# Cross-attention scores of a decoder layer: three float32r products of high and low parts, or one float32 product

## The chip, the cores and the metric

The kernel runs on one core of one Trainium2 chip. The metric is device time in microseconds (us) of that core, the median of several runs. The profile is of one further execution.

## The reference

One decoder layer over 8 requests of 128 tokens with 128 features: causal self-attention with 16 heads of 64, cross-attention with 16 heads of 8 on a context of 128 tokens, and a feed-forward of 8 experts with 256 hidden values of which two are chosen per token. After each of the three comes a residual and a layer norm. What the change touches is the cross-attention:

```python
qh = _split_heads(q @ Wq.T + bq, B, S)      # B=8, S=128, 16 heads of 8
kh = _split_heads(k @ Wk.T + bk, B, S)
vh = _split_heads(v @ Wv.T + bv, B, S)
scores = jnp.einsum('bhqd,bhkd->bhqk', qh, kh) / np.sqrt(DK)
scores = jnp.where(mask[:, None, :, :] == 0, NEG, scores)
attn = jax.nn.softmax(scores, axis=-1)
out = jnp.einsum('bhqk,bhkd->bhqd', attn, vh)
```

## The kernel before

Every engine has its own instruction stream, with the order of all calls written out by hand (there is no planner); semaphores tie the streams together. The attention of the 8 requests runs as a software pipeline: self-attention of request n, cross-attention of request n-1 or n-2 and the products of coming requests are interleaved call by call on each engine. After it the experts run in four chunks of 256 tokens. All eight PSUM banks (X0, X1, Y0, Y1, T0, T1, OS, OC) are handed from call to call by name; a call may write a bank once its last reader is done.

Many of the products are made from split operands: a value is held as a high part in float32r and a low part in float32r (value minus high part), and the product is the sum of three float32r products, high by high, high by low and low by high (`split_product`, lines 1441 to 1445; the projections at 1461 to 1465 and 1482 to 1484). Others, such as the transposes (L1545), the self-attention scores (L1527), the sums over keys (L1554 and L1563), the output projection (L1595) and the down products (L2043, L2053), are plain float32. In the trace each float32 product has two matmul records and two weight loads.

The cross scores, by which the change is told:

- `project_kc` (L1486, two calls) makes the keys of four requests at a time. `evac_kc` on ACT (L554) copies them to the high part `k_all[:, 0]` with their bias, and `lower_kc` on DVE (L823) writes the low part `k_all[:, 1]`. `k_all` lies in the memory of `down_sb`, the 1 MB of down weights, so that SP loads these weights only when the last of the 8 requests has used its keys (`sp.wait_ge(k_own_done, B)`, L272; the load is L273).
- `own_k` on POOL (L320) spreads the keys of one request, high and low part in one instruction each, over four column blocks and keeps in each block one head of each strip: `k_own`.
- `project_qc` (L1606) makes the queries of one request; `evac_qc` on DVE (L940) writes the high part `qc[:, 0]`, `lower_qc` on DVE (L828) the low part `qc[:, 1]`, out of the same bank.
- `score_c` on PE (L1538), 8 calls, one for each request: for each of four strips of 32 rows (8 features of 4 heads) three float32r products of 128 queries by 512 columns (4 heads by 128 keys) into the strip's own bank. That is 12 matmuls a call. It waits for `cq_evac`, `k_own_done` and `cq_lower`.
- `group_max` on DVE (L839) adds the mask to each strip's scores and takes the maxima; `exp` on ACT (L528) follows.

PE waits for `kc_lower` twice and for `cq_lower` once more ahead of calls that reuse a bank which `lower_kc` or `lower_qc` reads. DVE makes the mask (`spread_mask`, L818) once, from data that ACT's queue loads (L605); `x_tok`, which the residuals read, comes on the same queue (L609). SP's queue loads the weights: `gateT` and `upT` (L270, L271) are its last loads before `down`.

Of the kernel before, what the change touches and what calls it, by code (L numbers as in the profile page):

```python
# [5 lines left out]
F32 = mybir.dt.float32  # L6
F32R = mybir.dt.float32r
# [6 lines left out]
P = 128  # L14
# [24 lines left out]
def build_decoder(nc, x, xT, ctxT, mask, wqT, wkT, wvT, woT, cwqT, cwkT, cwvT, cwoT, cbq, cbk, cbv, cbo,  # L39
# [34 lines left out]
    with ExitStack() as ctx:  # L74
# [36 lines left out]

        k_all = down_sb[:].rearrange("p k d -> p (k d)").bitcast(F32R).rearrange("p (a t) -> p a t", a=2)

        ident = sb("ident", [P, P])
# [23 lines left out]
        ctx_lo = sb("ctx_lo", [P, B * S], F32R)  # L138
        k_own = sb("k_own", [P, 2, 2, 4, S], F32R)
        qc = sb("qc", [P, 2, S], F32R)  # L140
        cv_all = sb("cv_all", [P, B, D])
# [68 lines left out]
        def hid_of(b):  # L210
# [6 lines left out]
                             "bias_step bias_then_mean").split()]  # L217
        qk_first, qk_first_a, qk_first_v, kc_proj, kc_evac, kc_lower, cv_proj, cv_evac, k_own_done, cvp_done = [
            sem(n) for n in "qk_first qk_first_a qk_first_v kc_proj kc_evac kc_lower cv_proj cv_evac k_own_done cvp_done".split()]
        qk_proj, qk_evac = [[sem(f"{n}{i}") for i in range(4)] for n in ("qk_proj", "qk_evac")]  # L220
# [8 lines left out]
        (wo_s, res1_done, stat1_done, aggr1_done, var1_done, pow1_done, x1_ready, x1bo_done,  # L229
         x1T_ps, x1T_evac, cq_proj, cq_evac, cq_lower) = [sem(n) for n in (  # L230
             "wo_s res1_done stat1_done aggr1_done var1_done pow1_done x1_ready x1bo_done "
             "x1T_ps x1T_evac cq_proj cq_evac cq_lower").split()]
        (oc_evac, oct_ps, rec_c, ccat_done, ccatT_ps, ccatT_evac, wo_c, res2_done, stat2_done, aggr2_done, var2_done, pow2_done,
# [14 lines left out]
        @block.sync  # L248
        def _(sp):
            sp.dma_start(xT_all[:, 0:2 * S], xT[:, 0:2 * S]).then_inc(ld_xT, 16)  # L250
            sp.dma_start(w_raw[:, 1, W_COLS[0]], wkT[:, W_COLS[0]]).then_inc(ld_wqk[1], 16)
            for k in range(1, len(W_COLS)):
                sp.dma_start(w_raw[:, 0, W_COLS[k]], wqT[:, W_COLS[k]]).then_inc(ld_wqk[2 * k], 16)
            sp.dma_start(w_raw[:, 2, :], wvT).then_inc(ld_wv, 16)
            sp.dma_start(xT_all[:, 2 * S:B * S], xT[:, 2 * S:B * S]).then_inc(ld_xT_rest, 16)
            sp.dma_start(ctxT_all[:], ctxT).then_inc(ld_ctx, 16)
            sp.dma_start(cwqk_raw[:, 1], cwkT).then_inc(ld_cwk, 16)
            sp.dma_start(cwv_sb[:], cwvT).then_inc(ld_cw, 16)
            sp.dma_start(cwo_sb[:], cwoT).then_inc(ld_cw, 16)
            sp.dma_start(cb[:, 0], cbq).then_inc(ld_cw, 16)  # L260
            sp.dma_start(cb[:, 1], cbk).then_inc(ld_cw, 16)
            sp.dma_start(part[:], parts).then_inc(ld_cw, 16)
            sp.dma_start(cbrow[:, 0, :], cbv.rearrange("(a d) -> a d", a=1).broadcast_to([P, D])).then_inc(ld_cw, 16)
            sp.dma_start(cbrow[:, 1, :], cbo.rearrange("(a d) -> a d", a=1).broadcast_to([P, D])).then_inc(ld_cw, 16)
            sp.dma_start(router_sb[:], routerT).then_inc(ld_cw, 16)
            sp.dma_start(cwqk_raw[:, 0], cwqT).then_inc(ld_cwq, 16)
            sp.dma_start(wo_sb[:], woT).then_inc(ld_wo, 16)

            sp.wait_ge(w_lo_done, NWP)
            sp.dma_start(gu_raw[:, 0, :], gateT).then_inc(ld_gu, 16)  # L270
            sp.dma_start(gu_raw[:, 1, :], upT).then_inc(ld_gu, 16)  # L271
            sp.wait_ge(k_own_done, B)  # L272
            sp.dma_start(down_sb[:], down).then_inc(ld_down, 16)  # L273

            for c in range(NCH):
                for tb in range(TB):
                    b = c * TB + tb
                    sp.wait_ge(y_ready, b + 1)
                    sp.dma_start(out[b], y_out[:, tb, :]).then_inc(stored, 16)
            sp.wait_ge(stored, 16 * B)  # L280

        @block.gpsimd
        def _(pool):
# [30 lines left out]
            def own_k(n):  # L314

                for j in range(NG):
                    wait(pool, scored["c"][j], n - 1)
                pool.wait_ge(kc_lower, 1 + n // 4)
                for a in range(2):
                    last = pool.tensor_tensor(k_own[:, n % 2, a], spread(k_all[:, a, n * S:(n + 1) * S].bitcast(F32), 1, 4),  # L320
                                              spread(own[:], 2, S), ALU.mult)
                last.then_inc(k_own_done, 1)

# [183 lines left out]
        def _(act):  # L507
# [43 lines left out]
            def evac_kc(a, b):  # L551
                act.wait_ge(kc_proj, a + 1)
                act.wait_ge(bias_then_mean, 1)
                act.activation(k_all[:, 0, 4 * a * S:4 * (a + 1) * S], b[:], ACT.Identity,  # L554
                               bias=cb_nat[:, 1:2]).then_inc(kc_evac, 1)
# [242 lines left out]
        def _(dve):  # L798
# [20 lines left out]

            def lower_kc(a, b):  # L820
                hi = k_all[:, 0, 4 * a * S:4 * (a + 1) * S]
                dve.wait_ge(kc_evac, a + 1)
                dve.scalar_tensor_tensor(out=k_all[:, 1, 4 * a * S:4 * (a + 1) * S], in0=b[:], scalar=cb_nat[:, 1:2],  # L823
                                         in1=hi.bitcast(F32), op0=ALU.add, op1=ALU.subtract).then_inc(kc_lower, 1)

            def lower_qc(n, b):
                dve.wait_ge(cq_evac, n + 1)
                dve.scalar_tensor_tensor(out=qc[:, 1], in0=b[:, 0:S], scalar=cb_nat[:, 0:1], in1=qc[:, 0].bitcast(F32),  # L828
                                         op0=ALU.add, op1=ALU.subtract).then_inc(cq_lower, 1)

            def group_max(kind, g, n, b):
# [102 lines left out]
            def evac_qc(n, b):  # L934
                dve.wait_ge(cq_proj, n + 1)
                for j in range(NG):
                    wait(dve, scored["c"][j], n)
                if n == 0:
                    dve.wait_ge(bias_then_mean, 1)
                dve.tensor_scalar(qc[:, 0], b[:, 0:S], cb_nat[:, 0:1], None, ALU.add).then_inc(cq_evac, 1)  # L940

# [147 lines left out]
            evac_qk(1, 2, Y1)  # L1089
            lower_kc(0, OS)  # L1090
            reciprocal_s(3, 1)
# [3 lines left out]
            reciprocal_s(2, 1)  # L1095
            lower_kc(1, T1)
            group_max("s", 0, 2, OC)
# [4 lines left out]
            evac_qc(0, Y0)  # L1102
            lower_qc(0, Y0)
            evac_qk(1, 3, OC)
# [16 lines left out]
            evac_turned("s", 1, 2, T1)  # L1121
            lower_qc(1, X0)
            reciprocal_s(2, 2)
# [21 lines left out]
            evac_qc(2, T1)  # L1145
            lower_qc(2, T1)
            evac_turned("s", 1, 3, Y0)
# [24 lines left out]
            evac_qc(3, Y0)  # L1172
            lower_qc(3, Y0)
            evac_turned("s", 1, 4, Y1)
# [24 lines left out]
            evac_qc(4, X0)  # L1199
            lower_qc(4, X0)  # L1200
            normalise_x2(1)
# [27 lines left out]
            reciprocal_s(3, 6)  # L1229
            lower_qc(5, Y1)  # L1230
            evac_v(6, 0, T1)
# [28 lines left out]
            evac_x2T(2, T1)  # L1260
            lower_qc(6, Y0)
            reciprocal_s(3, 7)
# [15 lines left out]
            evac_qc(7, Y0)  # L1278
            lower_qc(7, Y0)
            evac_ccatT(5, X0)  # L1280
# [159 lines left out]
        def _(pe):  # L1440
# [90 lines left out]
            def score_c(m, *banks):  # L1531
                pe.wait_ge(cq_evac, m + 1)
                pe.wait_ge(k_own_done, m + 1)
                pe.wait_ge(cq_lower, m + 1)
                for j in range(NG):
                    rows = slice(32 * j, 32 * (j + 1))
                    for q, k in ((0, 0), (0, 1), (1, 0)):
                        last = pe.matmul(banks[j][:], qc[rows, q], k_own[rows, m % 2, k].rearrange("p s t -> p (s t)"),  # L1538
                                         start=(q == k), stop=(q == 1))
                    last.then_inc(scored["c"][j], 1)  # L1540

# [122 lines left out]
            score_s(2, 0, OC, Y1)  # L1664
            pe.wait_ge(kc_lower, 1)
            mix_s(1, 0, OS)
# [6 lines left out]
            turn_x1(0, T0)  # L1673
            pe.wait_ge(kc_lower, 2)
            next_qk(2, 2, T1)
# [34 lines left out]
            mix_c(1, 0, OC)  # L1710
            pe.wait_ge(cq_lower, 2)
            mix_s(2, 0, X0)
# [165 lines left out]
            score_s(7, 0, Y0, X0)  # L1878
            pe.wait_ge(turned_evac["c"][2], 5)
            score_c(5, T0, OC, X1, Y1)  # L1880
            mix_c(2, 4, OS)
# [40 lines left out]
            mix_c(0, 5, X1)  # L1922
            mix_c(1, 5, X1)
            score_c(6, OC, Y0, T1, Y1)
            pe.wait_ge(cat_done[0], 8)
# [192 lines left out]
```

## Time and profile before

| | us |
|---|---|
| median of 3 runs | 233.56 |
| lowest and highest | 233.28, 233.65 |
| the profiled execution | 233.06 |
| its span in the profile | 231.0 |

The span is from the first to the last instruction of the program; 2.06 us of the profiled execution lie around it. Busy time of an engine is the union of its records, and a matmul's record goes on until its last result is out, while the next matmul of another has begun: so PE's busy share says little of how fast PE could go, and the distance from one start to the next says more. PE is the matmul, PEld its weight loads, DVE VectorE, ACT ScalarE, POOL GpSimd, SP SyncE.

### The profile page before, as it was taken

The page shows a single profiled execution, that of the slowest core. Times are in us where ns is not written, and L with a number is a line of the kernel's source. Part 1 is how long each engine was busy: PE and PEld are TensorE (multiplying, and loading weights), DVE is VectorE, ACT ScalarE, POOL GpSimd, SP SyncE. Part 2 cuts the span into 40 slices and gives each one's busy share as a digit, 9 for nine tenths or more (in the row PEclk, how much of TensorE's full clock was granted, in tenths as well). Part 3 has the DMA queues.
Part 4 walks back from the last instruction along what each step waited for, and adds up shares of the span by engine and source line. Part 5 has one row for each costly group of instructions (what it writes and reads, how often), then busy time and mean ns, then how long its engine had stood idle before and what let it go on. Part 6 is the DMA issues. An engine that isn't in the chain of part 4 may idle for free.

```text
span 231.0 us, 6982 instructions
## 1 busy us (share of the span) xinstructions
PE 225.9 (98%) x2274; PEld 205.9 (89%) x2274; DVE 192.1 (83%) x954; ACT 164.9 (71%) x552; POOL 102.0 (44%) x162
## 2 busy tenths in 40 slices
PE   8999999999999999999999999999999999999992
PEld 8999888997978988978978988789999999999992
DVE  3897798997889889989899879989898565766984
ACT  3768988898999979999989999697476333333001
POOL 4387738796396568922978351231200000100112
PEclk9999999999999999999999999999999999999999
DMA  6998000000000000000002200000000000000000
GB/s 189 362 363 314 10 0 0 4 3 1 3 1 3 0 6 3 0 3 1 1 4 64 121 3 3 3 0 4 0 3 0 1 3 0 4 23 0 26 23 24
DMA packets 7011, 9.10 MB, mean 39 GB/s; under 512 B 1088, under 2 KB 5824, under 8 KB 6592
## 3 DMA queue, kind: packets, MB, share of 16 engines
q1 hardware_dynamic: 4320, 7.09, 8.7%
q10 hardware_dynamic: 2656, 1.57, 2.3%
q8 instruction: 18, 0.29, 0.5%
q14 instruction: 17, 0.14, 0.2%
HBM read 8.14 MB, written 0.52 MB: 37 GB/s over the span
## 4 chain that ended last, share of the span: by engine, by line
PE 96%; DVE 1%; issue 1%; POOL 1%; ACT 0%; POOLq 0%; ACTq 0%; DVEq 0%
PE bank L1545 13%; PE bank L1443 11%; PE bank L1445 10%; PE bank L1444 10%; PE bank L2043 9%; PE bank L1527 7%; PE bank L1554 7%; PE bank L1595 6%; PE bank L1563 4%; PE bank L1538 3%; PE bank L1611 2%; PE bank L1482 2%; PE bank L1483 2%; PE bank L1484 2%; PE bank L1570 2%; PE bank L2053 1%
## 5 line engine op out<-in xcount | busy, mean ns | idle before, releaser
L525 ACT ACTIVATE probs_s<-masked_s,nmax_s 128x128 f32<-128x128 f32 x128 | 49.8, 396 | 3.6 <-DVE nmax_s L839 2.1
L311 POOL TENSOR_TENSOR probs_s<-probs_s,rec_sum_s 128x512 f32<-128x512 f32 x32 | 33.1, 1040 | 35.0 <-DVE rec_sum_s L846 34.8
L586 ACT ACTIVATE silu<-bank 128x256 f32<-128x256 f32 x54 | 20.1, 384 | 30.3 <-PE bank L1445 28.4
L528 ACT ACTIVATE probs_c<-masked_c,nmax_c 128x128 f32<-128x128 f32 x128 | 40.3, 396 | 1.6 <-DVE nmax_c L839 1.4
L1443 PE MATMUL bank<-ctx_hi,gu_hi 128*128 128x256 f32 x128 | 38.7, 302 | 0.0
L1444 PE MATMUL bank<-ctx_lo,gu_hi 128*128 128x256 f32 x128 | 35.7, 279 | 0.0
L1445 PE MATMUL bank<-ctx_hi,gu_lo 128*128 128x256 f32 x128 | 35.7, 279 | 0.0
L839 DVE CUSTOM_DVE_ANT_0 masked_c<-bank,mask_add 128x128 f32<-128x128 f32 x128 | 29.0, 286 | 4.6 <-PE bank L1538 3.9
L839 DVE CUSTOM_DVE_ANT_0 masked_s<-bank,causal 128x128 f32<-128x128 f32 x128 | 29.2, 285 | 1.2 <-PE bank L1527 1.0
L503 POOL TENSOR_TENSOR mv<-mv,minus_half 128x1 f32<-128x1 f32 x7 | 3.8, 556 | 55.2 <-DVE mv L1388 55.2
L1443 PEld LDWEIGHTS bank<-ctx_hi,gu_hi 128*128 128x128 f32 x128 | 24.3, 190 | 0.7 <-DVE qk_a L969 0.3
L525 ACT ACTIVATION_READ_ACCUMULATOR probs_s<-masked_s,nmax_s 128x1 f32 x128 | 24.8, 193 | 0.0
L1444 PEld LDWEIGHTS bank<-ctx_lo,gu_hi 128*128 128x128 f32 x128 | 24.1, 188 | 0.0
L1445 PEld LDWEIGHTS bank<-ctx_hi,gu_lo 128*128 128x128 f32 x128 | 24.0, 188 | 0.0
L567 ACT COPY xT_all<-bank 128x512 f32<-128x512 f32 x32 | 17.8, 580 | 2.6 <-PE bank L1545 1.5
L1545 PE MATMUL bank<-ident,probs_c 128*128 128x128 f32 x128 | 18.8, 275 | 0.0
L1545 PE MATMUL bank<-ident,probs_s 128*128 128x128 f32 x128 | 18.7, 276 | 0.0
L1443 PE MATMUL bank<-x_hi,w_hi 128*128 128x256 f32 x62 | 18.2, 293 | 0.0
L969 DVE TENSOR_TENSOR qk_a<-silu,bank 128x256 f32<-128x256 f32 x32 | 12.7, 419 | 6.5 <-ACT silu L586 6.2
L1554 PE MATMUL bank<-probsT_s,v_sb 128*64 128x128 f32 x256 | 17.5, 279 | 0.0
L1445 PE MATMUL bank<-x_hi,w_lo 128*128 128x256 f32 x62 | 17.3, 279 | 0.0
L1444 PE MATMUL bank<-x_lo,w_hi 128*128 128x256 f32 x62 | 17.3, 279 | 0.0
(180 smaller groups left out, 591.4 us busy)
## 6 DMA issues: line engine op xcount, KB each, us to landing
raw<-in_gateT SPq DMA_DIRECT2D x1, 1024.0 KB, 8.2
raw<-in_upT SPq DMA_DIRECT2D x1, 1024.0 KB, 12.1
down_sb<-in_down SPq DMA_DIRECT2D x1, 1024.0 KB, 5.2
raw<-in_wvT SPq DMA_DIRECT2D x1, 512.0 KB, 5.6
ctxT_all<-in_ctxT SPq DMA_DIRECT2D x1, 512.0 KB, 6.9
masked_c<-in_mask ACTq DMA_DIRECT2D x1, 512.0 KB, 11.9
wo_sb<-in_woT SPq DMA_DIRECT2D x1, 512.0 KB, 6.1
x_tok<-in_x ACTq DMA_DIRECT2D x1, 512.0 KB, 11.2
```

The costliest lines, as they stand in the source:

```text
L311: pool.tensor_tensor(probs_s[:, g % 2], probs_s[:, g % 2], spread(rec_sum_s[:, 4 * g:4 * g + 4], 2, S), ALU.mult).then_inc(normed[g], 1)
L525: last = act.activation(probs_s[:, g % 2, i, :], masked_s[:, g % 2, i, :], ACT.Exp, scale=-1.0, bias=nmax_s[:, h:h + 1], accum_out=rsum_s[ ...
L528: last = act.activation(probs_c[:, g % 2, i, :], masked_c[:, g % 2, i, :], ACT.Exp, scale=-1.0, bias=nmax_c[:, h:h + 1])
L567: act.copy(dst[:, g % 2].rearrange("p h t -> p (h t)"), b[:]).then_inc(turned_evac[kind][g], 1)
L586: act.activation(silu[:, i % NS, :], g, ACT.Silu).then_inc(silued, 1)
L839: last = dve.tensor_tensor_reduce(out=masked[:, g % 2, i, :], in0=b[:, i * S:(i + 1) * S], in1=add, scale=-1.0, scalar=3e38, op0=ALU.add, ...
L1443: pe.matmul(dst, wh, xh, start=True, stop=False)
L1444: pe.matmul(dst, wh, xl, start=False, stop=False)
L1445: return pe.matmul(dst, wl, xh, start=False, stop=True)
L1545: last = pe.transpose(b[:, i * S:(i + 1) * S], (probs_s if kind == "s" else probs_c)[:, g % 2, i, :], ident[:])
L1554: last = pe.matmul(b[DQ * r:DQ * (r + 1), i * S:(i + 1) * S], v_sb[:, 8 * a + 2 * i + r, :], probsT_s[:, r, i, :], start=True, stop=True)
L2043: last = pe.matmul(down_bank(ce)[:, tb * P:(tb + 1) * P], hid[c % 2][:, e * FB + fb, tb * P:(tb + 1) * P], down_sb[:, e * FB + fb, :], sta ...
```

## The change

The keys and the queries of the cross-attention are held once, in float32. `score_c` makes one float32 product for each strip, which is two passes of 512 columns, 8 matmul records a call. `lower_kc` (2 calls) and `lower_qc` (8 calls) are gone with their semaphores and PE's waits for them. `own_k` has one instruction a request and waits for ACT's copy. `k_all` gets memory of its own, so that SP no longer waits for `k_own_done` and issues the load of `down` right after that of `upT`. Two waits are added on PE, ahead of `score_c(5)` and `score_c(6)`: for the copies out of the banks that these calls take, which the wait for `cq_lower` had covered. All other calls stand in the same order.

```diff
-        k_all = down_sb[:].rearrange("p k d -> p (k d)").bitcast(F32R).rearrange("p (a t) -> p a t", a=2)
-        k_own = sb("k_own", [P, 2, 2, 4, S], F32R)
-        qc = sb("qc", [P, 2, S], F32R)
+        k_all = sb("k_all", [P, B * S])
+        k_own = sb("k_own", [P, 2, 4, S])
+        qc = sb("qc", [P, S])
@@ SP
             sp.dma_start(gu_raw[:, 1, :], upT).then_inc(ld_gu, 16)
-            sp.wait_ge(k_own_done, B)
             sp.dma_start(down_sb[:], down).then_inc(ld_down, 16)
@@ POOL, own_k
-                pool.wait_ge(kc_lower, 1 + n // 4)
-                for a in range(2):
-                    last = pool.tensor_tensor(k_own[:, n % 2, a], spread(k_all[:, a, n * S:(n + 1) * S].bitcast(F32), 1, 4),
-                                              spread(own[:], 2, S), ALU.mult)
-                last.then_inc(k_own_done, 1)
+                pool.wait_ge(kc_evac, 1 + n // 4)
+                pool.tensor_tensor(k_own[:, n % 2], spread(k_all[:, n * S:(n + 1) * S], 1, 4), spread(own[:], 2, S),
+                                   ALU.mult).then_inc(k_own_done, 1)
@@ ACT, evac_kc: writes k_all[:, 4 * a * S:4 * (a + 1) * S]
@@ DVE
-            def lower_kc(a, b): ...
-            def lower_qc(n, b): ...
-                dve.tensor_scalar(qc[:, 0], b[:, 0:S], cb_nat[:, 0:1], None, ALU.add).then_inc(cq_evac, 1)
+                dve.tensor_scalar(qc[:], b[:, 0:S], cb_nat[:, 0:1], None, ALU.add).then_inc(cq_evac, 1)
-            lower_kc(0, OS)
-            lower_kc(1, T1)
-            lower_qc(0, Y0)
...
@@ PE, score_c
-                pe.wait_ge(cq_lower, m + 1)
                 for j in range(NG):
                     rows = slice(32 * j, 32 * (j + 1))
-                    for q, k in ((0, 0), (0, 1), (1, 0)):
-                        last = pe.matmul(banks[j][:], qc[rows, q], k_own[rows, m % 2, k].rearrange("p s t -> p (s t)"),
-                                         start=(q == k), stop=(q == 1))
-                    last.then_inc(scored["c"][j], 1)
+                    pe.matmul(banks[j][:], qc[rows, :], k_own[rows, m % 2].rearrange("p s t -> p (s t)"),
+                              start=True, stop=True).then_inc(scored["c"][j], 1)
@@ PE, order of calls
-            pe.wait_ge(kc_lower, 1)
...
-            pe.wait_ge(kc_lower, 2)
...
-            pe.wait_ge(cq_lower, 2)
...
+            pe.wait_ge(turned_evac["s"][1], 7)
             score_c(5, T0, OC, X1, Y1)
...
+            pe.wait_ge(x2T_evac, 3)
             score_c(6, OC, Y0, T1, Y1)
```

## Rows read from the trace of the kernel before

**Rows 1.** The profile page: the chain that ended last, by engine.

```profile
PE 96%; DVE 1%; issue 1%; POOL 1%; ACT 0%; POOLq 0%; ACTq 0%; DVEq 0%
```

**Rows 2.** Stage from:to, length; busy us of PE, PEld, DVE, ACT, POOL; granted clock.

```profile
40.00:148.00 108.00, 107.99 (x1217) 93.12 (x1211) 96.58 (x577) 100.21 (x356) 66.99 (x87) 1.00 0.04 12
```

**Rows 3.** Waits of PE's weight loads: us in total, times, longest.

```profile
PEld bank L1563 <- issue: 1.9, 10, 0.4
...
PEld bank L1527 <- ACT xT_all L567: 0.7, 2, 0.4
```

**Rows 4.** The chain in order of time (start, us, what): score_c, two plain float32 groups.

```profile
39.52 0.92 PE bank L1538 x12
...
43.83 1.31 PE bank L1545 x12
...
212.57 7.14 PE bank L2043 x64
```

**Rows 5.** PE's timeline, 52.7 to 54.0 us (start, us, what), and at 53.5 alone.

```profile
52.76 0.99 PE L1538 MATMUL bank<-k_own,qc 32*128 32x512 f32 x12
53.68 0.55 PE L1545 MATMUL bank<-ident,probs_s 128*128 128x128 f32 x3
...
53.32 0.43 PE L1538 MATMUL bank<-k_own,qc 32*128 32x512 f32 x4
```

**Rows 6.** PE's timeline, 57.9 to 58.5 us: float32r passes of 512 and 256 columns.

```profile
57.97 0.40 PE L1484 MATMUL bank<-w_hi,x_lo 128*128 128x512 f32 x1
58.20 0.28 PE L1443 MATMUL bank<-x_hi,w_hi 128*128 128x256 f32 x1
58.32 0.28 PE L1444 MATMUL bank<-x_lo,w_hi 128*128 128x256 f32 x1
```

**Rows 7.** Matmuls by line: duration in ns, min/median/max, first and last start.

```profile
L1538 PE MATMUL bank<-k_own,qc x96: 383/392/500, 39.5 to 147.3; 32*128 32x512 f32 x96
...
L1443 PE MATMUL bank<-x_hi,w_hi x62: 277/281/385, 6.2 to 108.8; 128*128 128x256 f32 x62
...
L1545 PE MATMUL bank<-ident,probs_c x128: 271/273/329, 43.7 to 156.1; 128*128 128x128 f32 x128
...
L1587 PE MATMUL bank<-router_sb,x2T_cur x16: 170/256/277, 122.2 to 164.2; 128*128 128x8 f32 x16
```

**Rows 8.** PE's timeline: float32 in four column strips, and in two row strips.

```profile
54.70 0.65 PE L1563 MATMUL bank<-xT_all,cvp 128*32 128x128 f32 x16
...
55.28 1.16 PE L1527 MATMUL bank<-qk_b 64*128 64x128 f32 x16
```

**Rows 9.** Groups by shape (count, busy us, mean ns): what leaves POOL and DVE.

```profile
L320 POOL TENSOR_TENSOR k_own<-down_sb,own 128x512 fp32r<-128x512 f32 x16 | 16.3, 1041 | 0.0
...
L828 DVE SCALAR_TENSOR_TENSOR qc<-bank,cb_nat,qc 128x128 fp32r<-128x128 f32 x8 | 2.8, 345 | 0.2
...
L823 DVE SCALAR_TENSOR_TENSOR down_sb<-bank,cb_nat,down_sb 128x512 fp32r<-128x512 f32 x2 | 1.5, 732 | 0.0
```

**Rows 10.** What DVE waited for: us in total, times, longest.

```profile
DVE masked_c L839 <- PE bank L1538: 3.9, 6, 1.4
```

**Rows 11.** DMA issues of the page (KB, us to landing), and the mask's issue time.

```profile
down_sb<-in_down SPq DMA_DIRECT2D x1, 1024.0 KB, 5.2
...
masked_c<-in_mask ACTq DMA_DIRECT2D x1, 512.0 KB, 11.9
...
9.42 0.39 ACTq L605 DMA_DIRECT2D masked_c<-in_mask  x1
```

**Rows 12.** DMA queues between 16 and 20 us: packets, MB, share of 16 engines.

```profile
q1 hardware_dynamic: 203, 1.53, 92.8%
q10 hardware_dynamic: 169, 0.08, 7.6%
```

**Rows 13.** DVE's timeline around the mask, 24.8 to 27.9 us.

```profile
25.11 0.69 DVE L818 TENSOR_SCALAR mask_add<-masked_c 128x1024 bf16<-128x1024 int32 x1
26.29 0.18 DVE L846 RECIPROCAL rec_sum_s<-rsum_s 128x4 f32<-128x4 f32 x1 [0.50 <-ACT probs_s L525]
```

More of the change, by code:

```diff
@@ L217, in build_decoder @@
                              "bias_step bias_then_mean").split()]
-        qk_first, qk_first_a, qk_first_v, kc_proj, kc_evac, kc_lower, cv_proj, cv_evac, k_own_done, cvp_done = [
-            sem(n) for n in "qk_first qk_first_a qk_first_v kc_proj kc_evac kc_lower cv_proj cv_evac k_own_done cvp_done".split()]
+        qk_first, qk_first_a, qk_first_v, kc_proj, kc_evac, cv_proj, cv_evac, k_own_done, cvp_done = [
+            sem(n) for n in "qk_first qk_first_a qk_first_v kc_proj kc_evac cv_proj cv_evac k_own_done cvp_done".split()]
         qk_proj, qk_evac = [[sem(f"{n}{i}") for i in range(4)] for n in ("qk_proj", "qk_evac")]
@@ L229, in build_decoder @@
         (wo_s, res1_done, stat1_done, aggr1_done, var1_done, pow1_done, x1_ready, x1bo_done,
-         x1T_ps, x1T_evac, cq_proj, cq_evac, cq_lower) = [sem(n) for n in (
+         x1T_ps, x1T_evac, cq_proj, cq_evac) = [sem(n) for n in (
              "wo_s res1_done stat1_done aggr1_done var1_done pow1_done x1_ready x1bo_done "
-             "x1T_ps x1T_evac cq_proj cq_evac cq_lower").split()]
+             "x1T_ps x1T_evac cq_proj cq_evac").split()]
         (oc_evac, oct_ps, rec_c, ccat_done, ccatT_ps, ccatT_evac, wo_c, res2_done, stat2_done, aggr2_done, var2_done, pow2_done,
@@ L553, in evac_kc @@
                 act.wait_ge(bias_then_mean, 1)
-                act.activation(k_all[:, 0, 4 * a * S:4 * (a + 1) * S], b[:], ACT.Identity,
+                act.activation(k_all[:, 4 * a * S:4 * (a + 1) * S], b[:], ACT.Identity,
                                bias=cb_nat[:, 1:2]).then_inc(kc_evac, 1)
@@ L818, in spread_mask @@
                 dve.tensor_scalar(mask_add[:], mask_all, 0.0, NEG, ALU.is_equal, ALU.mult).then_inc(mask_set, 1)
[L820 to L829, printed above, removed]
             def group_max(kind, g, n, b):
@@ L1145, in _ @@
             evac_qc(2, T1)
-            lower_qc(2, T1)
             evac_turned("s", 1, 3, Y0)
@@ L1199, in _ @@
             evac_qc(4, X0)
-            lower_qc(4, X0)
             normalise_x2(1)
@@ L1229, in _ @@
             reciprocal_s(3, 6)
-            lower_qc(5, Y1)
             evac_v(6, 0, T1)
@@ L1260, in _ @@
             evac_x2T(2, T1)
-            lower_qc(6, Y0)
             reciprocal_s(3, 7)
@@ L1278, in _ @@
             evac_qc(7, Y0)
-            lower_qc(7, Y0)
             evac_ccatT(5, X0)
```

2 lines of the change are left out of this document (removed).

## The prediction

> **What bounds the kernel now.** I read first the page's chain of work that ended last: 96% of the span is PE [rows 1]. A chain of PE alone can mean two things: PE has work without a break, or its records run into each other and hide small waits. So I read the stages next. From 40 to 148 us, where the attention of the eight requests is interleaved and where all calls of `score_c` but the first lie, PE is busy for 107.99 of 108 us at a granted clock of 1.00, the 2.4 GHz level, while DVE is at 96.58 and ACT at 100.21 [rows 2]. Last I read what PE's weight loads waited for. Nearly all of it is a fraction of a microsecond at a change from one way of using the array to another, put down to "issue" (ten times, 1.9 us in all, for L1563), which no other engine can shorten; waits for ACT or DVE are single cases of at most 0.4 us each (the largest group has two), with the same change of use inside them [rows 3]. I put what another engine truly holds back at under 0.5 us in the whole span. So a nanosecond added on PE is a nanosecond of the kernel, and what DVE, ACT or POOL are spared is worth next to nothing. The reader is to see that DVE at 89% of a stage is not a bound when PE is at 100% of it.
>
> **The change on PE, step by step.** A call of `score_c` stands in the chain with 0.92 us [rows 4]; there are eight, 96 records, the last of them at 147.3 us [rows 7]. Inside the call at 52.76 us twelve matmuls start in three rounds of four: all four strips run beside each other, the third round starts at 53.32, and the next group of PE at 53.68, which is again 0.92 us after the first start [rows 5]. What a round costs is read from float32r passes of 512 columns that follow each other: one starts at 57.97 and what follows it at 58.20, 0.23 us later; three rounds of this are 0.70 us (0.233 each, inside the two decimals), and the rest of the call, 0.22 us, is the way in and the way out, which stay [rows 5, 6].
>
> There is no float32 pass of 512 columns in this trace, so its price is bounded. Twelve float32 records of 128 columns take 1.31 us in the chain, 109 ns each; 64 of another line take 7.14 us, 112 ns each [rows 4]. A float32r pass of 256 columns has the duration of a float32 pass of 128, 281 against 273 ns: a float32 column costs what two float32r columns cost. By the column: float32r goes from 281 to 392 ns for 256 more columns, 0.43 ns each; float32 goes from 170 ns (8 columns, the shortest) to 273 ns (128 columns), 0.86 ns each [rows 7]. So 512 columns in float32 cost about four times 109 ns. If a small part of each pass is fixed the price is lower: the 512-column float32r pass costs 0.233 and the 256-column one 0.117 (58.20 to 58.32 us [rows 6]), a factor of 1.99, and that factor twice on 109 ns gives 0.432 us. I take 0.432, since it uses a measured lengthening of a pass. The ends are 0.42 (a larger fixed part) and 0.446 us (four times the 112 ns of L2043).
>
> Strips: float32 runs beside itself too. Sixteen records in four column strips take 0.65 us and sixteen in two row strips 1.16 us, the last record's 0.27 us included, where one after another they would take 1.75 (16 x 0.109) [rows 8]. So I count two rounds of four strips.
>
> The sum for a call: 0.22 + 2 x 0.432 = 1.08 us, against 0.92, so +0.165 us. Eight calls: +1.3 us. With the ends of the pass, 2 x 0.42 - 0.70 = +0.14 and 2 x 0.446 - 0.70 = +0.19, so +1.1 to +1.5 us. The four weight loads of a round start together and lie beside the matmuls of the round before, as now; one round of them fewer frees nothing, because only the first is exposed.
>
> The size by the pages: the Trainium skill ("FP8 and Floating Point Precision", TensorE Precision Notes) has true float32 make four passes through the array, which speaks against this change: four passes stand in place of three. With the gap of its page "TensorE: Matmul & The Clock Gate" (Back-to-back issue gap), N/2.4 + 2.5 ns, as an estimate a pass of 512 columns is 216 ns and the call grows by one such pass, +1.7 us over eight calls. The trace has 0.23 us for the float32r pass, more than that formula, which makes the old form dearer and the loss smaller; my sum goes by the trace.
>
> **The change on the other engines.** `lower_qc` takes 8 x 345 ns and `lower_kc` 2 x 732 ns off DVE, 4.3 us; half of `own_k`'s sixteen instructions go from POOL, 8.3 us [rows 9]. These lie beside PE's work, and I cost the relief at nothing: PE waits for DVE by under 0.5 us in all [rows 3], and that is the most that it can give back. The other way round, DVE waited 3.9 us for the scores of L1538 [rows 10]; each call brings its scores 0.165 us later, but DVE comes to it 0.35 us richer by the missing `lower_qc`. If DVE's lateness should reach PE all the same, the price is this 0.165 us once more per call; I don't expect it. ACT's copy of the keys keeps its form. The two waits added ahead of `score_c(5)` and `score_c(6)` are for copies that stand ahead of the old `lower_qc` in DVE's order, so they end no later than the wait that is gone; behind them queues all of PE, and the cost is nothing. The removed waits of PE for `kc_lower` and `cq_lower` end no idle time in the rows of waits, so they give nothing.
>
> **The load that moves.** `down`, 1 MB, went out when the last keys were used; now it follows `upT` at once, on the same queue. It is itself needed only by the down products, behind all attention. What it meets is the mask and `x_tok` on ACT's queue. While SP's queue has work the two share badly: from 16 to 20 us SP's queue (q1) moves 1.53 MB and ACT's (q10) 0.08 MB [rows 12]. The mask, issued at 9.42, lands after 11.9 us, at 21.3 us [rows 11]. One more megabyte at 1.6 MB in 4 us is 2.6 us more of this, so the mask lands near 24 us, and DVE reads it at 25.11 with nothing waiting there now [rows 12, 13]. The cover is about 1.1 us, and behind it DVE has 0.50 us of idle time at 26.29 [rows 13]. `x_tok`, behind the mask on ACT's queue, is first read by `residual1(0)`, ten calls further in DVE's order. I cost the load at nothing, and come back to it below.
>
> **The rivals.**
> (a) *The early load holds the mask up.* If SP's queue is served alone for as long as `down` took by itself, 5.2 us [rows 11], the mask lands at 26.5, `spread_mask` starts 1.4 us late, and DVE, which works in order, brings the next v and maxima late. The 0.5 us of idle time takes a part; up to 0.9 us reach PE. Time: 234.9 + 0.9 = 235.8. The Trainium skill ("DMA: Bandwidth & Descriptors", Arbitration) has an engine go round between its queues by packets; here the shares in rows 12 show what that does to the smaller packets.
> (b) *Float32 strips don't overlap over rows.* If the eight passes go one after another, a call costs 0.22 + 8 x 0.432 = 3.7 us, +2.8 us, and the kernel takes 233.56 + 22 = 256 us. Against it stand the row strips of L1527 [rows 8].
> (c) *The other side: faster.* The 109 ns of a float32 pass could be the weight load's price and not the columns': then a pass of 512 columns would stream at the float32r rate, 0.233 us, two rounds would replace three, and the change saves 8 x 0.233 = 1.9 us, 231.7. It decides if the streaming of 128 columns takes less than about 100 ns. Against it: L1563 loads 32 columns instead of 128, and its four rounds still take 0.38 us and the tail [rows 8]; and the durations grow with the streamed columns at 0.86 ns each, at an equal load [rows 7].
> (d) *The relief counts.* If nearly all waits of PE for DVE and ACT go, 0.5 us and a little more, the net is under +0.5 us of 233.56, which is no difference. It needs PE to be held more often than rows 3 show.
> (e) *It doesn't do what it says:* a float32 product of 512 columns becomes more than two passes. The float32 lines of rows 4 have two records a product; nothing points to more.
>
> **How the numbers follow.** The profiled execution took 233.06 us with 231.0 of span; the sum moves its span to 232.3. The median of the runs is 0.5 us above that execution, and I add the sum to the median: 233.56 + 1.3 = 234.9. A measurement of this kernel tells about 0.2%, 0.47 us, from no change. Chances: forecast with its bounds 0.83 (slower); (a) 0.05 (slower); (b) and (e) 0.02 (slower); (c) 0.03 (faster); (d) 0.07 (same). Slower 0.89, of which a hundredth or so goes to no difference by the scatter of the runs: 0.88; same 0.08; faster 0.04. Range: the low end is the smallest sum, +1.1, less half a microsecond for (d), 234.2; the high end is +1.5 with the start of (a) or a second 0.165 us in two or three calls, 235.7.
>
> **What would show it.** In the profile after: L1538 with 64 records of about 0.6 us each instead of 96 of 0.39; each call 1.08 us in the chain; PE's busy time up by the same 1.3 us in the stage from 40 to 148 us, its length with it; DVE and POOL down by 4.3 and 8.3 us with the end unmoved by it; waits for L1538 on DVE about as before; `down` landing before 30 us and `spread_mask` at 25 us with no wait. I am wrong if second starts inside a call come after 0.23 us (rival c), if DVE shows idle time before L818 (rival a), or if the stages from 148 us on change their length.

## The result

| | before | after |
|---|---|---|
| median of 13 runs, us | 233.51 | 234.02 |
| lowest and highest | 233.01, 233.99 | 233.42, 234.21 |
| the profiled execution, us | 233.06 | 234.06 |
| its span | 231.0 | 232.3 |

The change makes the kernel slower: the ratio is 1.0023, with a 95% interval of 1.0013 to 1.0032, which is +0.5 us (0.3 to 0.75). The forecast was 234.9 us and a range from 234.2 to 235.7: the direction is right, the time is 0.18 us below the range and the loss less than half of the 1.3 us that were forecast. Yet the span of the profiled execution grew by just these 1.3 us, and the next parts say why the two differ.

The page of the kernel after: instructions, busy time, the chain by engine.

```profile
span 232.3 us, 6895 instructions
...
PE 227.1 (98%) x2242; PEld 204.6 (88%) x2242; DVE 188.2 (81%) x944; ACT 165.0 (71%) x552; POOL 94.3 (41%) x154
...
PE 96%; DVE 1%; issue 1%; POOL 1%; ACT 0%; POOLq 0%; ACTq 0%; DVEq 0%
```

The chain is the same as in [rows 1]. DVE has 3.9 us less to do and POOL 7.7, and the chain's shares don't move. `score_c` is now L1511. Its durations by line, then the chain of after in order of time (start, us, what):

```profile
L1511 PE MATMUL bank<-k_own,qc x64: 587/640/692, 39.8 to 148.3; 32*128 32x512 f32 x64
```

```profile
39.89 1.07 PE bank L1511 x8
...
53.34 1.07 PE bank L1511 x8
...
147.86 1.07 PE bank L1511 x8
```

Each of the eight calls stands with 1.07 us where [rows 4] have 0.92 for the first. Inside the second one (PE's timeline at 53.5 us and at 54.15 to 54.3, in place of [rows 5]):

```profile
53.27 0.71 PE L1511 MATMUL bank<-k_own,qc 32*128 32x512 f32 x4
...
53.81 0.61 PE L1511 MATMUL bank<-k_own,qc 32*128 32x512 f32 x4
54.35 0.33 PE L1517 MATMUL bank<-ident,probs_s 128*128 128x128 f32 x1
```

Two rounds of four strips, 0.53 us from the first to the second (the way in of 0.11 is in it) and 0.54 us on to the next group. Added up over the eight calls, from the first start of a call to the first start of what follows it, the records give 8.57 us after and 7.39 us before: +1.18 us. That part of the sum is right to a tenth.

**Where the waits went.** PE's timeline around the turn of x1 (L1600 before, L1572 after), first before, then after:

```profile
64.31 0.40 PE L1484 MATMUL bank<-w_hi,x_lo 128*128 128x512 f32 x1
64.62 0.33 PE L1600 MATMUL bank<-ident,x 128*128 128x128 f32 x1
```

```profile
64.97 0.40 PE L1459 MATMUL bank<-w_hi,x_lo 128*128 128x512 f32 x1
65.20 0.31 PE L1572 MATMUL bank<-ident,x 128*128 128x128 f32 x1
```

Before, 0.31 us lie between the two starts; after, 0.23, which is the pass itself. So PE had waited 0.08 us for a `group_max` of DVE. No row of PE's matmuls shows it, and the row of the weight load in front has 0.3 us in both kernels. Laying the two traces side by side, matmul by matmul, finds the same at 104.25 us (0.08), about 105.6 (0.07) and a few of 0.03. From the first start of `score_c` to the end of the last down product PE takes 187.41 us before and 188.29 after: +0.88, so 0.30 us of the 1.18 come back as waits that are gone.

What lies behind these three waits is a pause of DVE inside a `group_max`, once for the first and once for the other two. The four instructions of a call start 0.21 us apart; here is DVE's timeline before, then PE behind it:

```profile
103.00 0.29 DVE L839 CUSTOM_DVE_ANT_0 masked_s<-bank,causal 128x128 f32<-128x128 f32 x1 [0.32 <-PE bank L1527]
...
103.48 0.29 DVE L839 CUSTOM_DVE_ANT_0 masked_s<-bank,causal 128x128 f32<-128x128 f32 x1
...
103.69 0.28 DVE L839 CUSTOM_DVE_ANT_0 masked_s<-bank,causal 128x128 f32<-128x128 f32 x1
...
104.25 0.50 PE L1482 MATMUL bank<-w_hi,x_hi 128*128 128x512 f32 x1
```

0.48 us lie between the first two starts, 0.27 more than between the others, and the call has no wait in between. The other pause, 0.09 us, ends at 64.05 us. Behind each, 0.6 us later, the instruction queue (q14) loads 8 KB. The kernel after has neither pause; it has one of 0.16 us at 143.1 us. So what makes PE wait at 64, 104 and 105.6 us before is a pause of DVE that falls elsewhere after, and whether DVE's spared work has a part in it must come from experiments.

**The start.** The rest of the +1.3 us of span lies ahead of `score_c`, and all of it is there by 15 us, before `lower_kc` or any other changed work of PE, DVE or POOL. PE's first passes of 256 columns, before and after:

```profile
5.77 0.28 PE L1465 MATMUL bank<-x_hi,w_lo 128*128 128x256 f32 x1
5.89 0.28 PE L1461 MATMUL bank<-x_hi,w_hi 128*128 128x256 f32 x1
```

```profile
6.48 0.41 PE L1440 MATMUL bank<-x_hi,w_lo 128*128 128x256 f32 x1
6.69 0.37 PE L1418 MATMUL bank<-x_hi,w_hi 128*128 128x256 f32 x1
6.90 0.28 PE L1419 MATMUL bank<-x_lo,w_hi 128*128 128x256 f32 x1
```

Starts 0.12 us apart are the 2.4 GHz level, 0.21 us apart the 1.2 GHz level. The trace's clock record rises at 5.67 us before and at 6.87 us after, both behind the same twenty warming matmul records. Five more passes at half the clock cost half a microsecond; with the other waits of the start, 0.36 us of it are left when `score_c` begins. The Trainium skill ("TensorE: Matmul & The Clock Gate", Part 1) lets the moment differ from run to run by half a microsecond either way; here it differs by 1.2 us between two executions. The rise alone doesn't set the start: in another kernel below (small POOL) the clock rose at 5.53 us and `score_c` begins at 39.99, behind a wait of 0.48 us at 7 us.

**The early load** did as expected. The mask's DMA in the page of after (issued at 9.79 us), and DVE's timeline around 25 us:

```profile
down_sb<-in_down SPq DMA_DIRECT2D x1, 1024.0 KB, 13.2
...
masked_c<-in_mask ACTq DMA_DIRECT2D x1, 512.0 KB, 14.4
```

```profile
25.47 0.68 DVE L814 TENSOR_SCALAR mask_add<-masked_c 128x1024 bf16<-128x1024 int32 x1
26.66 0.18 DVE L831 RECIPROCAL rec_sum_s<-rsum_s 128x4 f32<-128x4 f32 x1 [0.51 <-ACT probs_s L521]
```

The mask lands at 24.2 us instead of 21.3, and DVE reads it at 25.47 with no idle time ahead of it. The cover was thin: 1.3 us.

### The profile page after: what moved, and what is told of

The parts are those of the page before. It is cut to its first block, busy times and chain, and to the rows that moved or that the text cites. A ratio compares the mean times of both kernels' runs of the same rounds, so it can differ in the third digit from the quotient of the medians.

```text
span 232.3 us, 6895 instructions
## 1 busy us (share of the span) xinstructions
PE 227.1 (98%) x2242; PEld 204.6 (88%) x2242; DVE 188.2 (81%) x944; ACT 165.0 (71%) x552; POOL 94.3 (41%) x154
## 4 chain that ended last, share of the span: by engine, by line
PE 96%; DVE 1%; issue 1%; POOL 1%; ACT 0%; POOLq 0%; ACTq 0%; DVEq 0%
PE bank L1517 13%; PE bank L1418 10%; PE bank L1419 10%; PE bank L1420 10%; PE bank L2014 9%; PE bank L1502 7%; PE bank L1526 7%; PE bank L1567 6%; PE bank L1535 4%; PE bank L1511 4%; PE bank L1583 2%; PE bank L1457 2%; PE bank L1459 2%; PE bank L1458 2%; PE bank L1542 2%; PE bank L2024 1%
## 5 line engine op out<-in xcount | busy, mean ns | idle before, releaser
L1419 PEld LDWEIGHTS bank<-ctx_lo,gu_hi 128*128 128x128 f32 x128 | 24.2, 189 | 0.0
```

What stands on the lines that cost most here:

```text
L1419: pe.matmul(dst, wh, xl, start=False, stop=False)
```

## The experiments

All runs are compared with runs of the kernel before on the same chip. Three numbers are read from each: the ratio; the mean span of its runs, and what lies around it (the run's time less its span); and one time from its trace, PE from the first start of `score_c` to the end of the last down product, which leaves the start out. This last one comes from a single execution. In the four traces whose work behind `score_c` is that of before (before twice, `pos_e` on DVE, more POOL) it goes from 187.24 to 187.66 us, so a difference of a tenth or two is to be read with care.

| kernel | ratio (95%) | mean span | around it | `score_c` to end | POOL instructions |
|---|---|---|---|---|---|
| before, again | 0.9998 (0.9988 to 1.0009) | 231.25 | 1.99 | 187.42 | 162 |
| after, again | 1.0027 (1.0016 to 1.0039) | 232.06 | 1.82 | 188.15 | 154 |
| late down | 1.0032 (1.0019 to 1.0045) | 232.18 | 1.80 | 188.32 | 154 |
| DVE refilled | 1.0064 (1.0048 to 1.0081) | 232.98 | 1.79 | 188.44 | 154 |
| relief only | 0.9993 (0.9984 to 1.0002) | 231.03 | 2.02 | 187.16 | 162 |
| two passes | 0.9960 (0.9947 to 0.9972) | 230.47 | 1.98 | 186.44 | 162 |
| POOL refilled | 1.0048 (1.0036 to 1.0060) | 232.40 | 1.98 | 188.30 | 162 |
| product only | 1.0035 (1.0022 to 1.0049) | 232.12 | 2.04 | 188.47 | 162 |
| one own_k | 1.0028 (1.0018 to 1.0037) | 232.19 | 1.79 | 188.18 | 154 |
| after, small POOL | 1.0037 (1.0023 to 1.0052) | 232.26 | 1.99 | 188.34 | 162 |
| pos_e on DVE | 0.9997 (0.9986 to 1.0008) | 231.18 | 1.80 | 187.24 | 154 |
| more POOL | 1.0001 (0.9990 to 1.0013) | 231.44 | 1.79 | 187.66 | 178 |

### Both kernels again

No edit; is the small difference of the medians chance, or does a part of it lie outside of the span?

> The kernel before, unchanged, for its spans. The profile of the changed kernel has a span of 232.3 us against 231.0, which is the +1.3 us of the sum, but the medians differ by 0.5 us only. Theory A (chance): the moment at which TensorE's granted clock rises differs between executions, and the one profiled execution of before had an early one (5.7 us, against 6.9 us in the profile of after); then the spans of this kernel scatter by up to 1 us, their median is near 231.4 to 231.8, and what lies around the span is about 1.8 us as in the runs of after. Theory B (a part outside of the span): the kernel before has more around its span, 2.06 us in its profiled execution against 1.75 to 1.87 in thirteen of after; then the spans are near 231.0 to 231.5 and the rest stays near 2.06 us in each.

> The changed kernel, unchanged, beside it on the same chip. Ratio to before 1.0023 again (+0.3 to +0.75 us). Theory A: where the clock rises at the same time as in the profile of before, the trace lies 0.85 us behind before's at the end (eight calls of score_c at 0.15 us, less 0.3 us of waits that went), not 1.3. Theory B: span minus span is about +0.9 and the part around the span 0.25 us smaller.

Both theories hold a part. The spans of the kernel before scatter from 230.9 to 231.8 us over 11 runs (from 230.8 over 26 more), so the profiled execution with 231.0 was one of the early ones. And what lies around the span differs: 1.99 and 2.01 us in these two sets of the kernel before, 1.82 us in 11 runs of after. So the mean time moves by +0.83 us of span (232.06 against 231.23) less 0.18 us around it, +0.66 (0.19 with the thirteen runs of after in the result). In the second trace of after the way from `score_c` to the end is 0.73 us longer than before's.

### The early load

```diff
@@ after
+            sp.wait_ge(k_own_done, B)
             sp.dma_start(down_sb[:], down).then_inc(ld_down, 16)
```

> The changed kernel with the load of the down weights back behind the wait for the last keys. If the early load costs anything (mask landing late, shared queues at the start) this one is faster than the changed kernel, by 0.1 to 0.5 us; if the early load gains by anything it is slower. My theory: no difference, below 0.1 us, since the mask landed at 24.2 us and DVE read it with nothing waiting.

No difference that these runs can tell: the intervals overlap, the time from `score_c` to the end is that of after. A cost of the load below some 0.2 us would not show.

### DVE's relief

```diff
@@ after: at each place of lower_qc once, of lower_kc twice
+            spare_op()    # spare = (ident + 1.0) - ident, 128 columns
```

> The changed kernel with twelve extra DVE instructions of 128 columns (some 0.3 us each) at the places where lower_qc and lower_kc stood; they work on a spare tile and nobody waits for them. Relief theory: the short waits of PE for DVE (0.07 us at 64.6, 0.08 at 104.3, 0.06 near 105.6 us) come back and this kernel is 0.2 to 0.35 us slower than the changed one, +0.8 us against before. Rival (the relief is worth nothing, all is PE's own): same as the changed kernel within 0.1 us.

Slower than after, by 0.9 us of mean span, more than expected; but this edit is not a faithful one. The spare instructions by tile:

```profile
L821 DVE SCALAR_TENSOR_TENSOR spare<-ident x12: 259/282/1053, 31.6 to 147.4; 128x128 f32<-128x128 f32 x12
```

One of them, which reads and writes SBUF only, took 1.05 us instead of 0.28, while POOL was at work. `lower_qc` reads PSUM and never took over 0.35 us. The trace, of the fastest of the six runs, has PE's wait at the turn of x1 back (0.18 us at 65 us, behind a pause of 0.17 us in DVE's `group_max`), but from `score_c` to the end it is only 0.1 to 0.3 us longer than those of after, so most of the 0.9 us stands in no kept trace. The run shows that instructions added on DVE cost time, not how much the relief is worth. Two cleaner edits come from the other side. The first takes the relief alone: `score_c` multiplies high parts only, in three passes as before, and the result lacks the low parts; the waits for `kc_lower` become waits for `kc_evac`, and the two waits that the change adds on PE are there too.

```diff
@@ before
-            lower_kc(0, OS)
...
-            lower_qc(7, Y0)
-                        last = pe.matmul(banks[j][:], qc[rows, q], k_own[rows, m % 2, k].rearrange("p s t -> p (s t)"),
+                        last = pe.matmul(banks[j][:], qc[rows, 0], k_own[rows, m % 2, k].rearrange("p s t -> p (s t)"),
```

> The kernel before with DVE's part of the change alone: lower_kc and lower_qc are gone, and score_c makes its three float32r passes all from the high parts (so the scores lack their low parts). PE's records and POOL's instructions are as many as before. If the relief is worth what the trace of after shows (the waits of PE at 64.6, 104.3 and near 105.6 us go, -0.2 to -0.35 us in the span), this kernel is 0.3 to 0.5 us faster than before. If the part around the span (2.00 us before, 1.81 after) goes with the two semaphores fewer, it is 1.8 us here; if it goes with the PE records, 2.0 us. If the relief is worth nothing: no difference from before.

Its trace has the expected 0.25 us less between `score_c` and the end, and PE's timeline at the turn of x1 has lost its wait (0.24 us between the starts, where before has 0.31):

```profile
64.38 0.40 PE L1474 MATMUL bank<-w_hi,x_lo 128*128 128x512 f32 x1
64.62 0.31 PE L1589 MATMUL bank<-ident,x 128*128 128x128 f32 x1
```

The mean span is 0.16 to 0.2 us shorter, and the whole is too small for the ratio to tell. Nor does it show that DVE's relief is the cause. The kernel `pos_e` on DVE, further below, has all of DVE's work of before in this stage and only eight memsets more at DVE's start; its time from `score_c` to the end is 187.24 us, and its PE has lost the same wait:

```profile
64.59 0.40 PE L1485 MATMUL bank<-w_hi,x_lo 128*128 128x512 f32 x1
64.83 0.31 PE L1601 MATMUL bank<-ident,x 128*128 128x128 f32 x1
```

The pauses in DVE's `group_max` tell the two apart from before. In the six traces with DVE's stream as before (before twice, two passes, product only, one own_k, more POOL) they fall at 64 and 104 us; in the six traces without `lower_qc` and `lower_kc` and with nothing in their place there is one, at 142 to 143 us; with `pos_e` on DVE they fall at 44.6 and 139 us. So they go with the place in DVE's instruction stream. The relief can't be had without moving that stream, and no run here parts the two.

The second edit does the opposite, the float32 product with nothing else:

```diff
@@ before: k_all, k_own and qc in float32; lower_kc, lower_qc, own_k, all waits and loads as they were
-                    for q, k in ((0, 0), (0, 1), (1, 0)):
-                        last = pe.matmul(banks[j][:], qc[rows, q], k_own[rows, m % 2, k].rearrange("p s t -> p (s t)"),
-                                         start=(q == k), stop=(q == 1))
+                    last = pe.matmul(banks[j][:], qc[rows, 0], k_own[rows, m % 2, 0].rearrange("p s t -> p (s t)"),
+                                     start=True, stop=True)
```

> The kernel before with the float32 product alone: keys and queries in float32, one product for each strip, while lower_kc, lower_qc, both instructions of own_k, all waits and the late load of the down weights stay. My theory now: the sum of the prediction holds for this one. PE from the first score_c to its last record takes 1.18 us more than before (188.6 us instead of 187.41), since no relief of DVE gives anything back, and the part around the span stays at 2.0 us; so +1.1 to +1.3 us against before, and 0.5 to 0.6 slower than the changed kernel. Rival (relief and POOL's instructions have nothing to do with it): as the changed kernel, +0.5 to +0.65 us.

The calls take 8.57 us, +1.18 as in after. From `score_c` to the end it is +1.06: even with all of DVE's work in place 0.12 us of waits vanish. The wait at the turn of x1 is still there; those at 104 and 105.6 us are nearly gone, though DVE pauses there as before (0.24 us); why is not shown. With DVE's relief (after, and three kernels like it: 188.15 to 188.34) it is +0.73 to +0.93. The measured time, ratio 1.0035 (+0.5 to +1.1 us), is below the expected 1.1 to 1.3 at its centre and overlaps both theories. Its mean span is 0.83 us above that of before on the same chip (231.30), and after's is 0.84 above that of before on its own (231.22). So the order of sizes comes from the traces alone, and the spans of the runs don't show that the relief gave anything.

### Is PE one for one?

```diff
@@ before
-                    for q, k in ((0, 0), (0, 1), (1, 0)):
+                    for q, k in ((0, 0), (1, 0)):
```

> The kernel before with two of the three float32r passes of score_c (high by low of the keys is left out; DVE and POOL still make all parts). PE is the bound at one for one: each call loses 0.231 us, the span -1.85 us. If DVE takes over as the bound once PE has less to do, it is less than that, -1.2 to -1.6 us. Part around the span: 2.0 us if semaphores decide it, near 1.8 if PE's records do.

It is not, in this direction. Six of the eight calls lose 0.23 to 0.25 us each, the first 0.07 and the fifth nothing: 1.52 us in all. From `score_c` to the end only 0.97 us are gained, and 0.72 us of mean span. PE's timeline at the fifth call and its follower:

```profile
101.49 0.75 PE L1538 MATMUL bank<-k_own,qc 32*128 32x512 f32 x8
102.44 0.38 PE L1527 MATMUL bank<-qk_a 64*128 64x128 f32 x2 [0.19 <-DVE qk_a L910]
```

0.95 us lie between these starts, as long as with three passes. PE now waits here for DVE's copy (L910), and in other places for ACT's copies (0.16 us at 41.4 and at 86.3); 0.22 us more lie at 72.9. So PE is the bound by a margin of tenths of a microsecond only: a nanosecond added counts nearly in full by the trace, 1.06 of 1.18 (0.83 by the mean span); a nanosecond taken away counts for about two thirds, 0.97 of 1.52, and for half of the 1.85 that were meant.

### What lies around the span

> The changed kernel with own_k's instruction made twice (POOL's relief undone, 8.3 us), and with two more semaphores, so that as many are taken as before. POOL's relief is worth nothing: the span as in the changed kernel (median 231.9 to 232.1 us) within 0.1 us. Part around the span: 2.0 us if the semaphores decide it, 1.8 if not. If POOL's relief counts, the span is longer by 0.2 to 0.4 us.

```diff
@@ after
-                pool.tensor_tensor(k_own[:, n % 2], spread(k_all[:, n * S:(n + 1) * S], 1, 4), spread(own[:], 2, S),
-                                   ALU.mult).then_inc(k_own_done, 1)
+                for _ in range(2):    # the second waits for the first, by a semaphore of its own
+                    last = pool.tensor_tensor(k_own[:, n % 2], spread(k_all[:, n * S:(n + 1) * S], 1, 4),
+                                              spread(own[:], 2, S), ALU.mult)
```

POOL's work costs nothing behind `score_c` (188.30 us, as after). Its five runs have a mean span 0.3 us longer than after's. Its one trace has a wait of PE of 0.37 us at 10 us, ahead of `score_c`; whether this is what the runs have stays open. Around the span lie 1.98 us instead of 1.82. The semaphores don't decide it: `e_relief_only` takes two fewer than before and has 2.02. That leaves the number of POOL's instructions, tried three ways:

```diff
@@ before (one own_k): both parts in one instruction of 1024 columns
-                for a in range(2):
-                    last = pool.tensor_tensor(k_own[:, n % 2, a], spread(k_all[:, a, n * S:(n + 1) * S].bitcast(F32), 1, 4),
+                pool.tensor_tensor(k_own[:, n % 2], spread(k_all[:, :, n * S:(n + 1) * S].bitcast(F32), 2, 4),
@@ after (small POOL)
+                pool.memset(pad8[:, n:n + 1], 0.0)
@@ before (pos_e on DVE): the eight memsets of L386 move to DVE's start
-                last = pool.memset(pos_e[:, :, e:e + 1], float(e - E))
+                last = dve.memset(pos_e[:, :, e:e + 1], float(e - E))
```

> The kernel before with own_k's two instructions made one over both parts, 8 POOL instructions fewer and the same work. In eight kernels so far the part around the span was 1.8 us where own_k has 8 instructions and 2.0 us where it has 16. If the number of POOL's instructions decides it, 1.8 us here with the span as before, -0.2 us in all; if it is anything else in the changed kernel, 2.0 us and no difference.

> The changed kernel with eight small POOL instructions more (a memset of one column after each own_k), so that POOL has as many instructions as before with almost none of the work. If the number decides it, the part around the span is 2.0 us; if POOL's work or its large instructions do, 1.8 us. The span as in the changed kernel in both.

> The kernel before with the eight memsets of pos_e (L386) moved from POOL to DVE, which has nothing to do then; nothing else. If the number of POOL's instructions sets the part around the span, it goes from 2.0 to 1.8 us at an unchanged span, and this kernel is 0.2 us (0.08%) faster than before. If own_k's instructions are special, 2.0 us and no difference.

1.79, 1.99 and 1.80 us: each falls to the side that the count of POOL's instructions says (154, 162, 154), whatever work these do. Is it in proportion to the count?

```diff
@@ before
+            for i in range(16):
+                pool.memset(pad16[:, i:i + 1], 0.0)
             split_x(0)
```

> The kernel before with sixteen small POOL memsets more at its start, where POOL waits for xT (its wait of 1.5 us takes them in). If the part around the span grows with the number of POOL's instructions in proportion (0.19 us for 8), it is 2.4 us here; if there is a step between 154 and 162 instructions, it stays at 2.0 us.

Neither: with 178 instructions it is 1.79 us again. (Its span is 0.2 to 0.3 us longer. Its trace has 0.24 us of that behind 172 us, spread over hundreds of the experts' matmuls; `pad16` also moves other tiles in SBUF, and neither was followed.) So the 0.19 us belong to particular lengths of POOL's instruction stream, and 162 is one of the dearer ones.

The traces have a sign that goes with it. DMA queues of before from 231 us to 236, behind its span:

```profile
q14 instruction: 1, 0.01, 0.6%
```

That is a load of 8 KB of instructions at 232.8 us, when the program's last instruction is over. All seven traces with 162 POOL instructions have one such load, 1.7 to 2.0 us behind the end of the span; the six with 154 and the one with 178 have none, and theirs is the short time around the span. Whether the load is what costs the time, or only comes with it, no run decides. For this change it means a gain of 0.19 us that has nothing to do with what the change computes.

`pos_e` on DVE is the only kernel with a mean time below before's on the strength of this: 232.98 us (12 runs) against 233.14 (23 runs). The ratio doesn't tell it from no change. The one kernel that is clearly faster than before, two passes, leaves a product out.

The span of the kernel with one long `own_k` grew by 0.9 us, for another reason. Instructions by line (ns min/median/max), `normalise_x1`, in before and there, and then the timeline there:

```profile
L869 DVE TENSOR_SCALAR x<-res,mv x8: 336/346/586, 34.2 to 144.1; 128x128 f32<-128x128 f32 x8
```

```profile
L867 DVE TENSOR_SCALAR x<-res,mv x8: 338/346/1439, 34.5 to 145.2; 128x128 f32<-128x128 f32 x8
```

```profile
114.09 3.74 POOL L319 TENSOR_TENSOR k_own<-down_sb,own 128x1024 fp32r<-128x1024 f32 x2
...
114.62 1.44 DVE L867 TENSOR_SCALAR x<-res,mv 128x128 f32<-128x128 f32 x1
...
116.12 0.33 PE L1598 MATMUL bank<-ident,x 128*128 128x128 f32 x1 [0.71 <-DVE x L867]
```

Here the DVE instruction, from SBUF to SBUF, stands still until POOL's instruction of 1.87 us is over, and PE waits 0.71 us for it. In before, with instructions of 1.04 us, the worst case is 0.59 us and PE's order covers it. The Trainium skill ("SBUF — State Buffer", SBUF: two separate sides) calls this the pair of ports that VectorE and GpSimd share, locked for a whole instruction; the trace agrees, with 1.44 us here. Instructions that read PSUM, `group_max` beside it, keep their 0.28 us.

## Why the direction was right and the size wrong

- **What bounds the kernel.** PE, yes: the chain and the stage are as read. But "a nanosecond added on PE is a nanosecond of the kernel" was too much (1.06 of 1.18 in the trace of the product alone, 0.83 in the mean span of its runs), and it doesn't hold for one taken away.
- **The pass and the call.** Forecast +0.165 us a call and +1.3 in all; measured +0.1475 and +1.18 [rows 5 against 53.27 to 54.35 us]. The float32 pass of 512 columns costs 0.43 us, as derived; three float32r rounds and their way in and out come to 0.923 and not 0.92. By the Trainium skill's four passes ("FP8 and Floating Point Precision", TensorE Precision Notes) at N/2.4 + 2.5 ns each ("TensorE: Matmul & The Clock Gate", Back-to-back issue gap) the estimate was +1.7. Four such passes are 0.86 us, and the trace agrees with two records of 0.43; what the trace has otherwise is the float32r pass, 0.23 us and not 0.216.
- **What comes back from DVE's side: the term that was put at nothing.** The step said: "I cost the relief at nothing", with 0.5 us as the most it could give back. In after 0.30 us of PE's waits are gone behind `score_c` (0.25 us with the relief alone, 0.12 with the product alone, together not their sum). I had read the rows of idle time, which don't price these waits: they are 0.03 to 0.08 us each, hidden in the tail of a matmul's record, and show only as a distance between starts that is longer than the pass. Rival (d) had such waits go, was set at 7%, and put it down to the relief. That is not shown: 0.22 of the 0.30 us are the three waits behind the two pauses of DVE, and these go as well where DVE's instructions are moved and not made fewer (`pos_e` on DVE). How much the 4.3 us of spared work are worth by themselves stays open.
- **DVE's wait for the scores** was to stay about the same. It went from 3.9 us [rows 10] to 6.6:

```profile
DVE masked_c L824 <- PE bank L1511: 6.6, 6, 1.7
```

  2.7 of the 4.3 us that DVE was spared it spends waiting for the scores. That is the sign that PE sets the pace here, and why 4.3 us of relief are worth 0.3 at most.
- **The part outside of the span: the term that was missing.** I took 2.06 us before as 2.06 us after. It is 0.19 us less, and this goes with the length of POOL's stream, which no step of the forecast looked at.
- **The sum with what was measured.** 1.18 for the calls, -0.30 for waits, -0.19 around the span: +0.69 us. The two measurements give +0.54 (0.30 to 0.75) and +0.63 (0.37 to 0.91). The agreement of the profiled span with the forecast, +1.3, was chance: 0.36 us of it are the later start. In the chances, slower adds up to 0.90 and not to 0.89, which changes nothing.
- **The load that moves**: right in its numbers. The mask landed at 24.2 us (forecast near 24) and nothing waited; rival (a) did not come. **Rivals (b) and (c)**: strips run beside each other, second starts come after 0.53 us. **(e)**: two records a product.

## What to carry to other kernels

Before a product of split float32r parts is replaced by one float32 product, count the passes with their measured price: for 512 columns three of 0.23 us against two of 0.43. By this case it can pay only where the splitting itself is on the path. When PE is "100% busy", measure the slack by distances between starts, matmul by matmul, against the plain distance of the same pair elsewhere; the table of idle time misses what hides in the tails. When such a wait ends at another engine, look whether that engine had work or paused inside one call; a pause moves with every instruction added or taken out ahead of it, and a small gain from an edit may be no more than that. And a difference below half a per cent needs the spans of many runs: one profile against one profile carried 0.4 us of a start that neither kernel decides.

## What the runs showed of the hardware

- A float32 matmul record of 512 columns in strips of 32 rows has its follower 0.43 us later, a float32r one 0.23 us, way in and way out left aside; four strips run at a time in both. For 128 columns in float32 it is 0.11 us [rows 4].
- The granted clock rose from its lower to its upper level between 5.03 and 7.20 us of the span over fourteen traces, behind the same warming matmuls.
- DVE paused 0.07 to 0.28 us inside a `group_max` in each trace, once or twice, always at the same places of its instruction stream: counted in the trace's records of DVE, at the 191st, 319th, 576th or 831st, which lie 128 or a multiple of it apart, give or take one. Behind each pause, 0.6 to 0.9 us later, came a load of 8 KB on the instruction queue.
- Time around the span: 1.8 us with 154 or 178 POOL instructions, 2.0 us with 162, in all twelve kernels measured; the dearer one also scatters more, from 1.84 to 2.15 in single runs of the kernel before, where those of after stay within 1.75 to 1.87. With 162, and only there, a load of instructions follows the end of the span.
- A DVE instruction from SBUF to SBUF (`normalise_x1`) waited out a POOL instruction of 1.87 us: it took 1.44 us instead of 0.35.
- While SP's queue moved packets of 8 KB, ACT's queue with its rows of 512 B got a twentieth of the bytes [rows 12]; a third megabyte on SP's queue moved the mask's landing by 2.8 us (24.2 us against 21.4 in late down).
